# Expert weights split into high and low parts beside six shared chunks, and routed blocks of three products in both feed-forwards

## What is computed

```
def _swiglu(x, w1, w2, w3):
    return jax.nn.silu(x @ w1) * (x @ w2) @ w3
...
scores = jax.nn.sigmoid(x @ router_w)
sel_scores = scores + expert_bias
_, top_idx = jax.lax.top_k(sel_scores, K)
top_scores = jnp.take_along_axis(scores, top_idx, axis=-1)
gates = jnp.sum(jax.nn.one_hot(top_idx, E, dtype=scores.dtype) * top_scores[..., None], axis=-2)
...
def body(acc, ws):
    w1, w2, w3, g = ws
    return (acc + _swiglu(xf, w1, w2, w3) * g[:, None], None)
```

## Time and profile before

| | us |
|---|---|
| median of 3 runs | 1652.69 |
| lowest and highest | 1650.48, 1654.33 |
| the profiled execution | 1648.27 |
| its span, first to last instruction | 1646.6 |
| mean granted clock of TensorE, of 1 | 0.964 |

### The profile page before, as it was taken

How to read it: one execution, slowest core, us unless ns; L and a number is a source line. 1 busy time by engine, 2 the same in 40 slices (tenths; PEclk the granted TensorE clock), 3 DMA queues, 4 the chain that set the end, 5 groups by cost and what they waited for, 6 DMA issues and landing times. The chain is left out here.

```text
span 1646.6 us, 27985 instructions
## 1 busy us (share of the span) xinstructions
PE 1517.7 (92%) x8708; PEld 1164.1 (71%) x8708; DVE 943.0 (57%) x1987; ACT 628.3 (38%) x1238; POOL 596.3 (36%) x831
## 2 busy tenths in 40 slices
PE   5999999999999966998999999965999999998998
PEld 5888885555558854666666666635788888887887
DVE  5477644455544755775666676514776455554566
ACT  2322223333322313655555655534223334433332
POOL 5428802323331005443553553333188223332100
PEclk9999999999999987998999999977999999999999
DMA  9749833655547524345445443325088343346751
GB/s 312 257 169 322 285 100 132 217 208 198 204 150 246 166 81 105 99 106 128 114 111 123 124 131 99 90 76 191 24 302 301 124 162 125 123 150 222 226 190 52
DMA packets 170559, 269.46 MB, mean 164 GB/s; under 512 B 20146, under 2 KB 124082, under 8 KB 168386
## 3 DMA queue, kind: packets, MB, share of 16 engines
q1 hardware_dynamic: 140386, 201.20, 39.3%
q0 software_dynamic: 19104, 56.64, 9.5%
q10 hardware_dynamic: 10944, 9.97, 2.0%
HBM read 129.52 MB, written 108.27 MB: 144 GB/s over the span
## 5 line engine op out<-in xcount | busy, mean ns | idle before, releaser
L1169 PE MATMUL f_bank<-f_xparts,f_sw 128*128 128x512 f32 x1536 | 381.8, 399 | 12.6 <-DVE f_sw L1082 9.3
L1169 PEld LDWEIGHTS f_bank<-f_xparts,f_sw 128*128 128x128 f32 x1536 | 285.8, 192 | 69.0 <-issue 12.2
L768 POOL DMA_INDIRECT outputs_by_choice<-f_yr,f_home x160 | 154.1, 963 | 400.6 <-DVE f_yr L1114 334.2
L1853 DVE TENSOR_REDUCE at_mx<-at_ps 128x1 f32<-128x384 f32 (+3 forms) x352 | 215.0, 633 | 140.7 <-PE at_ps L1993 140.3
L1766 ACT ACTIVATE at_pT<-at_ps 128x512 f32<-128x512 f32 (+1 forms) x352 | 194.4, 559 | 88.9 <-PE at_ps L2009 78.6
L1683 POOL TENSOR_SCALAR_AFFINE_SELECT at_pT<-at_pT 128x128 f32<-128x128 f32 (+2 forms) x352 | 124.6, 362 | 247.2 <-ACT at_pT L1766 243.6
L2009 PE MATMUL at_ps<-at_qT,at_kT 98*128 98x256 f32 (+3 forms) x512 | 174.3, 393 | 19.3 <-DMA at_qT<-at_mT 17.2
L736 POOL DMA_INDIRECT rows_by_slot<-f_xq,slot x128 | 142.6, 1114 | 119.9 <-issue 78.1
L795 ACT CAST f_hparts<-f_hid 128x512 fp32r<-128x512 f32 x128 | 79.3, 620 | 248.6 <-DVE f_hid L1033 248.6
L1286 PE MATMUL f_bank<-f_ew,f_hid 128*128 x320 | 157.6, 615 | 2.3 <-ACT f_hid L842 2.2
L1033 DVE TENSOR_TENSOR f_hid<-f_sil,f_bank 128x512 f32<-128x512 f32 x128 | 87.9, 686 | 123.0 <-PE f_bank L1169 114.8
(11 more groups left out here) (184 smaller groups left out, 2468.0 us busy)
## 6 DMA issues: line engine op xcount, KB each, us to landing
weights_in_parts<-f_stage SPq DMA_DIRECT2D x16, 1536.0 KB
f_ew<-outputs_by_choice SPq DMA_DIRECT2D x16, 1024.0 KB, 6.8
f_ew<-in_L_ffn_routed_w_dram SPq DMA_DIRECT2D x48, 256.0 KB, 6.9
f_whi<-weights_in_parts SPq DMA_DIRECT2D x16, 768.0 KB, 9.1
f_ring<-weights_in_parts SPq DMA_DIRECT2D x16, 768.0 KB, 4.6
f_rawx<-rows_by_slot SPq DMA_DIRECT2D x84, 128.0 KB, 5.0
rows_by_slot<-zero POOLq DMA_DIRECT2D x10, 1024.0 KB, 19.8
f_rawx<-rows_by_slot ACTq DMA_DIRECT2D x76, 128.0 KB, 2.1
```

The lines of the kernel that those rows point to most:

```text
L768: nc.gpsimd.indirect_dma_start(dram.yk, bass.IndirectOffsetOnAxis(ap=home[:, i:i + 1], axis=0), yr[:, i % 4, :], None).then_inc(y_st[i % 4 ...
L1169: ins = pe.matmul(ps[j % 2][:, :], sw12[:, wp, k, w, j * P:(j + 1) * P], xparts[:, u, xp, k, :], start=(i == 0), stop=(i == 3 * KD - 1))
L1853: v.tensor_reduce(own, ps1[i % RING1][:, 0:heads * w].rearrange("p (j a x) -> p j a x", a=min(heads, 2), x=w), AX.X, ALU.max).then_inc(mx_ ...
```

## The change

- Eight chunks are now cut six and two in the first feed-forward (`BEHIND = NC - 2`), five and three still in the second.
- In the first, ACT casts halves of an expert's weights (768 columns) in the steps of `PART_AT` and DVE subtracts in that step and the next. Raw weights lie in seven places (`PLACE`), four of them used three times, so that SP stores the low part (`store_low`), waits for its landing (`lo_st`) and then loads the next expert there. The high parts stay in `whi`.
- The routed stage of the first is now the one of the second (`step`): three products, high parts from `whi`, low parts from `ring`. SP stores the high parts there (`store_high`). ACT issues the fetches of blocks, as in the second.
- In both, SP issues the load of expert e before it waits for the landing of e - 1 (`load_low(e)`, then `low_in(e - 1)`).
- In both, marks have one buffer instead of two, and PE makes each inverting product one step earlier.
- In the first, the 16 half sums stand in 14 steps of the two chunks behind.
- SP loads the first four experts at the start, not after the routing.

```
-    BEHIND = NC - 3
+    BEHIND = NC - 3 if pre is None else NC - 2
...
+        PART_AT = [14, 16, 18, 20, 22, 24, 26, 28, 30, 32, 33, 35, 36, 38, 41, 45]
+        PLACE = [0, 1, 2, 3] * 3 + [4, 5, 6, 6]
...
             def load_expert(e):
+                if used_before(e):
+                    sp.wait_ge(lo_st[PLACE[e]], 16 * used_before(e))
...
+            def store_low(e):
+                sp.wait_ge(lo_made, 2 * e + 2)
...
+                sp.dma_start(dram.wparts[e * P:(e + 1) * P, EW:], lo.bitcast(F32)).then_inc(lo_st[PLACE[e]], 16)
...
+                store_low(2)
+                next_x(4)
+                load_expert(6)
+                for e in (3, 4):
+                    store_low(e)
+                    load_expert(e + 4)
+                store(2, U(2))
+                store_low(5)
+                next_res(4)
+                load_expert(9)
...
             for e in range(RING, E):
                 end = sp.value_load(ends_i[0:1, e - RING:e - RING + 1], min_val=1, max_val=NB)
                 sp.wait_ge(dn_done, end)
                 load_low(e)
-                low_in(e)
+                low_in(e - 1)
+                if not exact:
+                    store_high(e - RING)
+            low_in(E - 1)
+            if not exact:
+                for e in range(E - RING, E):
+                    store_high(e)
+                sp.wait_ge(hi_st, 16 * E)
...
             def chunk(c, c2, u, fresh, last):                   
                     nc.scalar.activation(sil[:, j % 2, :], psA[j % 2][:, :], ACT.Silu).then_inc(s_done, 1)
+                    if not exact and n in PART_AT:
+                        high_part(PART_AT.index(n), 0)
                     act.wait_ge(h_done, n + 3)
                     nc.scalar.copy(hparts[:, j % 2, 0], hid[:, j % 2]).then_inc(h_hi, 1)
+                    if not exact and n in PART_AT:
+                        high_part(PART_AT.index(n), 1)
...
+            def high_part(e, half):
+                if half == 0:
+                    act.wait_ge(raw_in[PLACE[e]], 48 * (used_before(e) + 1))
...
-                if i >= 2:
-                    dve.wait_ge(inv_done, i - 1)
+                if i >= 1:
+                    dve.wait_ge(inv_done, i)
...
-                    part = c * z.JS + j - INVERT_AT - 2
+                    part = c * z.JS + j - INVERT_AT - 1
...
+            if exact:
+                COMBINE_AT = [first + k for first in (3, 6, 8, 11, 14, 16, 19, 22) for k in range(TOPK)]
+            else:
+                COMBINE_AT = [2, 3, 4, 5, 6, 7, 8, 9, 10, 11, 12, 13, 13, 14, 14, 15]
```

More of the change, by code:

```diff
@@ new lines, in _ @@
+            if not exact:
+                store_low(15)
+                for s in range(4):
+                    sp.wait_ge(lo_st[s], 48)
+            sp.wait_ge(h_lo, BEHIND * z.JS - 1)
+            if not exact:
+                sp.wait_ge(lo_st[6], 32)
+            load_low(0)
+            sp.wait_ge(b_done, BEHIND * z.JS)
+            load_low(1)
+            sp.wait_ge(sh_st[1], 16 * (BEHIND // 2))
+            load_low(2)
+            low_in(0)
+            store(last, 0)
+            low_in(1)
@@ new lines, in _ @@
+            low_in(2)
+            sp.wait_ge(sh_st[0], 16 * (last // 2 + 1))
+            sp.wait_ge(h_lo, BEHIND * z.JS)
+            load_low(3)
+            if not exact:
+                for s in range(4, 6):
+                    sp.wait_ge(lo_st[s], 16)
+            for e in range(RING, E):
+                end = sp.value_load(ends_i[0:1, e - RING:e - RING + 1], min_val=1, max_val=NB)
+                sp.wait_ge(dn_done, end)
+                load_low(e)
+                low_in(e - 1)
+                if not exact:
+                    store_high(e - RING)
@@ L1029, in chunk @@
                     n = c * z.JS + j
+                    if not exact and n - 1 in PART_AT:
+                        low_part(PART_AT.index(n - 1), 1)
                     dve.wait_ge(s_done, n + 1)
@@ L1036, in chunk @@
                                     ).then_inc(h_lo, 1)
+                    if not exact and n in PART_AT:
+                        low_part(PART_AT.index(n), 0)
                     if j == 0 and not fresh:
@@ L1095, in step @@
                 i = q * 4 + r
-                if has(1) and not exact:
-                    dve.wait_ge(th_done, i)
-                    v.tensor_copy(hrT[:, (r - 1) % 2, :], rTh[:, 0:KR * P]).then_inc(hT_ev, 1)
-                if has(-1) and exact:
+                if has(-1):
                     low_rows(i + 1, (r + 1) % 2)
@@ L1104, in step @@
                                     ).then_inc(rh_done, 1)
-                if has(1) and exact:
+                if has(1):
                     dve.wait_ge(hT_hi, i)
@@ L1233, in weights_at, with step @@
                 e = pe.snap((words[i // DIGITS] >> (4 * (i % DIGITS))) & (E - 1))
-                if not exact:
-                    return [pe.snap(e * EW)]
                 return [pe.snap(e * EW), pe.snap(e + 1), pe.snap(((e * 3) & (RING - 1)) * EW)]
             at = {0: weights_at(0)}
-            def step_exact(q, r, has, u):
+            def step(q, r, has, u):
                 i = q * 4 + r
```

347 lines of the change are left out of this document (143 added, 204 removed).

## The result

The changed kernel takes 1633.5 us in the median (1632.4 to 1637.3), beside 1653.5 us for the kernel before. The ratio is 0.9886, with a 95% interval of 0.9863 to 0.9908, that is 19 us less (15 to 23). Measured once more it was 0.9871 (0.9850 to 0.9893). The forecast was 1621 in a range of 1609 to 1641: the direction and the range hold, and some 12 us of the expected 31.7 are missing. The profiled executions stand 13.7 us apart (1646.6 and 1632.9 us of span).

What follows compares the result with a forecast made beforehand. PE, busy 92% of the span, was taken as the bound. Terms of +2.5 +1.5 +1 -33.7 +2.5 (first) and +1.5 -7 (second) sum to -31.7: 1648.3 to 1616.6, or 1621 against the median; range 1609 to 1641, own range 1612 to 1631.

Steps and rivals of the forecast that it cites:

- The model of the stage: First routed stage: takes the second's pace, 209.5 us without its waits and clock loss; 224.5 us forecast, saving 33.7.
- The stores: First routed stage: ring loads with high-part stores between them make PE wait 10 us, plus 5 us for the clock.
- The order of the ring: Second routed stage: issuing each load before waiting for the landing ahead gives -7 us (0 to -10.7).
- The inverting product: Chunks of both feed-forwards: making it one step earlier costs +1.5 us in each.
- VectorE's lateness: Chunks of the first feed-forward: DVE's marks and added subtractions make it late in steps 13 to 28, +2.5 us.
- the expert traffic: Chunks of the first feed-forward: SP's store-then-load turns, taken as 10 us with 10.2 free, cost +1 us (0 to +18).
- Late weights: Rival, chance 0.17: SP's turn in the first feed-forward's chunks takes 12 us, ACT and PE wait; +15 us, 1636.
- The sign that I named for the lateness: First feed-forward's chunks: PE waits on ACT's h parts some 3 us in steps 16 to 28, none in 29 to 45.
- The chunks behind: Two chunks behind the first routed stage: doubled sums make DVE 2.2 us late; +2.5 us with closer last stores.
- over 74 us, the sums of y wait for their loads: Sign for the stage behind the first routed stage: longer than 74 us would mean y's sums wait for loads.
- The scatter: POOL, first feed-forward's chunks: contention with DVE subtractions could end it up to 30 us later; total same to 3 us worse.
- kept stalls: Rival, chance 0.12: the ring's order gives nothing in the second, stores cost 10 us more in the first; 1638.

Runs made afterwards that it cites:

- the sixth: Changed kernel with high-part stores early, inverting product later, and the residual made ahead of the expert's low part; 1606.9 us, ratio 0.9711.
- order-alone variant: Kernel before with only the wait for a ring load, in the second feed-forward, moved one load later; ratio 0.9933.

## Why the prediction was right, and where it wasn't

**The model of the stage was right.** The first routed stage without stores under its ring takes 211.3 to 213.3 us in five traces of six (mean 212.4), the second's pace; the sixth has 216.0. The prediction had 209.5 for that. The 2.9 us between are ring waits that stay also without stores (1.3 to 2.3 us in the five) and the clock behind them. That is the first mis-sized term: it took the second stage's ring waits off to zero. PE also waits 1.7 to 1.9 us before the chunks behind, but 1.4 us of such a wait stood at the end of the second stage before, and so lie in the 209.5.

**The stores were costed somewhat low, and left where they were.** The prediction gave the ring waits of this stage, for loads and stores together, 10 us and the clock 5. Measured, the stage is 20.3 and 18.0 us over the 209.5 in the two profiles of the changed kernel, and 17 and 15 of that go with the stores. The make is another: 7.8 us of ring waits (8.1 in the second profile), 1.5 for fetched rows, 3.84 at the end of the stage (2.83), and the clock behind these. Of the wait at the end only 1.4 us were in the 209.5, the rest was in no term. It comes through POOL: the scatters of y land late, and y's buffers come free late.

**The order of the ring** was sized right: -7 forecast, -6.2 in the changed kernel, -6.8 alone. Its worth in the first feed-forward, 9 to 11 us, was never written down, because the prediction costed the stage with the new order only. With the stores where the changed kernel has them, the whole gain hung on this edit.

**The inverting product** is the term that missed most for its size. The prediction put 1.5 us for each feed-forward, from the one place at 134.0, and said that the later sets end 0.8 us before PE asks. They don't: there were five waits in the first and three in the second. Over the five traces with the product early the chunks are 224.7 and 191.8 us in the mean, over the four with it late and the residual in its old place 220.9 and 188.1, the second being what before has (188.6 and 187.1). That is 3.8 and 3.7 us, where 1.5 and 1.5 were forecast. The step that failed was to count DVE's work against PE's over two steps. The marks are due within the step in which they are made.

**VectorE's lateness and the expert traffic** were forecast at 3.5 us together. With the product late, the chunks are 220.9 us against 217.9 for before and its order-alone variant (184.5 and the 33.4 of the moved steps): 3.0. SP's turn came out under what was free, with these stores of low parts in the timeline of the changed kernel, the first two and the ninth:

```profile
136.18 0.35 SPq L605 DMA_DIRECT2D weights_in_parts<-f_whi  x1
...
148.07 0.34 SPq L605 DMA_DIRECT2D weights_in_parts<-f_whi  x1
...
214.01 0.34 SPq L605 DMA_DIRECT2D weights_in_parts<-f_whi  x1
```

The first turn took 11.9 us, but the eight from 136.2 to 214.0 are 9.7 us each, under the 10.2 that are free. ACT never waited for an expert's load; it waited once for the landing of a store of a low part, 0.95 us at 237. Late weights did not happen. A subtraction of 768 columns took 0.95 us, as interpolated. The sign that I named for the lateness was not seen: of the 1.7 us in which PE waited for ACT's h parts, 1.38 stand at 119.1, and the kernel before has the same 1.38 at 119.4. The lateness showed in the marks, and as a residual 1.55 us late at 224.0, among the steps in which I expected nothing.

**The chunks behind** are 77.2 us in the mean of six traces with early stores or the later product and the sums as they were, 3.0 over the 74.2 that they would be; forecast 2.5. PE's only wait within the stage is 2.01 us at 586.1, for ACT's h parts in the last steps, where the doubled sums were costed at 2.2; no sum waited for y. So the sign "over 74 us, the sums of y wait for their loads" was drawn wrong: 74.2 is the stage without any lateness, under my own forecast of 76.7. The changed kernel's own 79.0 has 2 us more from the slow start behind the 3.84 us wait.

**The scatter.** By the first and last start of its 64 instructions, before and after (ns min/median/max between):

```profile
L736 POOL DMA_INDIRECT rows_by_slot<-f_xq,slot x64: 959/963/2148, 111.8 to 209.9; - x64
...
L799 POOL DMA_INDIRECT rows_by_slot<-f_xq,slot x64: 959/995/2158, 111.4 to 213.3; - x64
```

It ends 3.4 us later, and nothing waited for that: expert 14's load, which needs it, was issued at 241.9, behind other work of SP. The rule of the Trainium skill (GPSIMD Engine Reference, Specifications), contention with DVE instructions that have two SBUF inputs, had as much as 30 us in it; the trace agrees with its direction only (a median 32 ns longer), and one pair of traces hardly tells even that.

**The rivals.** 1633.5 us is above the forecast's own range (1612 to 1631) and near late weights (1636) and kept stalls (1638), but it is neither. The weights were in time, and of the kept stalls only the half about the stores is true: 3 to 5 us more than the term, where the rival had 10, while the order gave what it should. That 1633.5 lies in the outer range is in part luck: the range reached to 1641 to take in these two rivals, and what filled it were small terms that nearly all missed on the same side.

**The balance.** Against the forecast, the changed kernel's two profiles have +3.0 and +2.6 us in the first chunks, +5.3 and +3.0 in the first routed stage, +2.3 and +1.1 behind it, +1.6 and +2.5 in the second chunks, +0.8 and +0.6 in the second routed stage, +1.6 and -0.1 behind: 14.6 and 9.7 us, around the 12 that the medians miss. The attention adds +3.5 and -2.4, which no edit explains. What the clock does in it from run to run stays open.

## What to carry to other kernels

When work is moved out of a stage, look at when its transfers are issued and not only at how many there are: the 16 stores cost 15 to 17 us with 14 of them among the ring's loads, and nothing that shows in the 148 us before them, where the queues' share was 0.42. In an order of loads and waits on one queue, issue the next load before waiting for the last landing; here that small edit decided whether a large one gained anything. Due dates inside a step are to be laid against PE's own point in that step; a balance of busy times over two steps hides waits of one to three microseconds, each of which can also cost clock.

## What was not expected of the hardware

- A short wait of PE can cost as much again in clock, or nearly. Behind the 3.84 us wait, 24 products took 8.30 us where they take 5.8 at the 2.4 GHz level, 2.5 us more. With the stores early the wait there was 1.66 us, and the granted clock of 0.79 over the next 8.3 us is worth 1.7 us (an estimate, 0.21 x 8.3). It isn't regular, not even within one program: in the two executions of the changed kernel the chunks behind in the second feed-forward began after waits of 2.34 and 2.39 us, with a granted clock of 0.79 and of 1.00 over the next 8.2 us, and the same work took 108.0 and 106.3 us.
- The same attention took 517.1 to 527.3 us in the thirteen traces, 518.5 and 524.4 in two executions of one program. Over the whole kernel the two executions stand 11 us apart, so a single pair of profiles resolves no difference of that size.
- With eight stores of 768 KB in each long expert, at a share of 0.62 instead of 0.42, PE's 147.4 us were no longer than the 147.9 with two stores in all. At a share of 0.90 over 82 us, PE's busy time fell to 83%.
